# A decoder layer with a mixture of experts: the experts' outputs added into an accumulator in memory instead of stored in two halves

## The chip, the cores and the metric

The kernel runs on one core of a Trainium2 chip. The metric is the device time of one execution in microseconds (us). The core has five engines that run their own instruction streams and wait for each other on semaphores: TensorE (PE: matrix products, with its weight load PEld), VectorE (DVE), ScalarE (ACT), GpSimd (POOL) and SyncE (SP), which here only issues transfers (DMAs). POOL issues DMAs too, above all the indirect ones, whose row addresses come from a tile of indices. SBUF is the on-chip memory with 128 partitions.

## The reference

The input is x, 32 batches of 112 rows of 256 numbers (3584 rows, `NT`), and a context of 32 x 375 rows. A self-attention layer, a cross-attention layer with two subtracted softmaxes, and a mixture of experts follow each other. After each of them its input is added to its output and the sum is normalised to mean 0 and variance 1 per row (`_layernorm`, no weights). Only the last of them matters here:

```
h = normalised rows after cross-attention                      # [3584, 256]
scores = h @ gate_w.T                                          # 8 experts
mult1, mult2, idx = top-2 choice with two weights per row
y[row] = sum over the 2 chosen experts e of  mult_e * (silu(h @ w1[e].T) * (h @ w3[e].T)) @ w2[e].T
out = layernorm(h + y)
```

So each row of the output is a sum of three rows: h and the outputs of two experts.

## The kernel before

The program has four stages, one after another, with a barrier of all engines and a clearing of semaphores between them (`Phase.close`).

`front` computes self-attention, the first normalisation and the projections of the cross-attention, and leaves them in memory.

`cross` goes through the 32 batches. Each batch takes 24 steps (`PARTS`); the order is written out by hand, with tables that say in which step of which batch an engine does a piece. ACT writes the normalised rows h of batch b to `rows[:, b, 0:256]` (line 1005), in step 20 of the loop's batch b + 1, and signals `y_ready`. `rows` is an SBUF tile that lives to the end; beside the 256 numbers of h each row carries its own number (column 256), its first expert and its two weights. POOL scatters every row of a batch twice into the tensor `routed` in memory (line 916), sorted by expert. Rows between the experts' ranges are filled from the tile `pad` (lines 904 to 910), 256 rows by one DMA, nine DMAs in all, which SP issues at the end of the stage (lines 876 and 877); the first eight need a row address that the routing gives last. A padding row carries expert -1, weights 0 and a row number of 7168 or above. SP also feeds the loop: for each batch the two parts of the negated row maxima (`row`, line 858, after ACT's copy in line 978), and the loads of keys and queries (`load`). When c reaches 32, SP loads the first expert's weights into slot 0 of `w` (line 870, 3 MB), to be ready for the next stage.

`experts` works through 35 blocks of 256 sorted rows (two tiles of 128 rows, `BT`). Per block SP loads the rows (line 1403) and the expert's weights (line 1407, 3 MB, into one of two slots, issued once the block before has left that slot). PE turns the rows, multiplies by w1 and w3 in 8 pieces, and by w2 in 8 pieces, each as three half-precision products. DVE works out in `destinations` the share of each row and its destination `dest_i`: row number r for a row whose first choice this expert is, 3584 + r for the second choice, a place behind 7168 for a padding row. ACT scales the result into `y` (line 1465), and POOL scatters it tile by tile to the tensor `y` in memory (line 1427). No two scatters ever write the same row, so nothing orders them. The tile y has two slots, one per block in turn; DVE's `destinations` and ACT's scaling wait for the scatters of the block two before (`y_stored`).

`finish` reads both halves of `y` back, in 4 chunks of 8 batches, with 112 partitions. POOL adds the two halves (line 1628), DVE adds h from `rows` (line 1637) and takes the statistics (lines 1640 and 1644), POOL turns them into a scale and a shift (lines 1618 to 1624, of which 1620 is the power -0.5), ACT applies them (line 1651) and SP stores the chunk (line 1607).

The lines below are those that set the order in the last stage on POOL: the addition of a chunk stands before the statistics of the chunk before.

```
                for c in range(chunks):
                    pool.wait_ge(loaded[c], 32)
                    pool.tensor_tensor(y1[:, c], y1[:, c], y2[:, c], ALU.add).then_inc(half_sum, 1)
                    if c:
                        statistics(c - 1)
                statistics(chunks - 1)
```

## Time and profile before

| what | us |
|---|---|
| median of 3 runs | 1861.12 (1859.83 to 1864.59) |
| the profiled execution, its own time | 1862.62 |
| its span in the trace | 1860.7 |
| stage `finish`, from its first DMA issue to the end | 57.34 |
| PE busy | 1629.8 |
| DVE busy | 1153.1 |
| ACT busy | 915.8 |
| POOL busy | 747.5 |

The first three lines say how long the program takes; the profiled execution is 1.5 us above the median of the timed runs. The busy times are sums over all stages, so they say which engine sets the pace over most of the program (PE), and nothing on a single stage. All times of the trace count from the span's start.

### The profile page before, as it was taken

Reading aid. Unit: us, or ns where it says so; the run is one execution under the profiler, and the core shown is the slowest. Engines: PE = TensorE matmul, PEld = TensorE weight load, DVE = VectorE, ACT = ScalarE, POOL = GpSimd, SP = SyncE. Lnnn points to the kernel's source line nnn. Section 1 sums busy time; section 2 is a strip of 40 time slices with the busy share of each in tenths; the row PEclk is TensorE's granted clock in tenths of the full one; section 3 lists DMA queues with packets and bytes.
Section 4 is the critical chain, followed back from the end, with each engine's and each line's share of the span. In section 5 each row is a group of like instructions: output and inputs, shape, how many; then the busy total and the mean of one; then the engine's idle time right before and its main releaser. Section 6 shows DMA issues by size and latency. Waiting matters only on the chain. (4 is left out here: it accounts for less than half of the span.)

```text
span 1860.7 us, 46590 instructions
## 1 busy us (share of the span) xinstructions
PE 1629.8 (88%) x17724; PEld 1223.2 (66%) x17724; DVE 1153.1 (62%) x2648; ACT 915.8 (49%) x2168; POOL 747.5 (40%) x928
## 2 busy tenths in 40 slices
PE   4899999995999999999999998579999999999950
PEld 2666666663566666666665665368888888888840
DVE  5566666662888887788777888434444444444424
ACT  2344444443466666666666665434444444444423
POOL 6343343322755666765775576301111101111116
PEclk9999999997799999999999999779999999999985
DMA  6666666644444445555554453356555566666637
GB/s 174 186 188 172 177 187 176 181 112 97 136 139 138 131 125 145 145 140 136 147 166 124 132 150 98 127 199 238 224 220 222 223 228 237 238 238 228 220 88 184
DMA packets 204149, 317.11 MB, mean 170 GB/s; under 512 B 60600, under 2 KB 170840, under 8 KB 203928
## 3 DMA queue, kind: packets, MB, share of 16 engines
q1 hardware_dynamic: 188280, 247.16, 44.5%
q0 software_dynamic: 15648, 66.97, 10.2%
q8 instruction: 142, 2.33, 0.5%
q14 instruction: 79, 0.65, 0.1%
HBM read 225.84 MB, written 87.89 MB: 169 GB/s over the span
## 5 line engine op out<-in xcount | busy, mean ns | idle before, releaser
L1165 DVE TENSOR_REDUCE cross_mx<-cross_bank_max 112x2 f32<-112x750 f32 x512 | 460.7, 933 | 119.1 <-PE cross_bank_max L1245 116.4
L996 ACT ACTIVATE cross_probs<-cross_bank_score 125x448 f32<-125x448 f32 x768 | 406.5, 545 | 241.9 <-PE cross_bank_score L1235 238.9
L1556 PE MATMUL experts_bank_h<-experts_x_hi,w 128*128 128x256 f16 x2240 | 373.3, 274 | 1.4 <-DVE experts_x_lo L1477 1.4
L1556 PE MATMUL experts_bank_h<-experts_x_lo,w 128*128 128x256 f16 x1120 | 306.6, 274 | 0.0
L1514 DVE TENSOR_TENSOR experts_hid<-experts_bank_h,experts_gated 128x256 f32<-128x256 f32 x280 | 118.6, 424 | 285.5 <-ACT experts_gated L1453 285.4
L1235 PE MATMUL cross_bank_score<-cqst,ckst 97*125 97x448 f16 x768 | 283.9, 371 | 4.8 <-ACT cross_probs L996 2.4
L1245 PE MATMUL cross_bank_max<-ckst,cqst 96*112 96x375 f16 x1024 | 258.8, 335 | 28.2 <-DVE cross_mx L1165 21.2
L1427 POOL DMA_INDIRECT y<-experts_y,experts_dest_i x70 | 67.2, 960 | 510.1 <-ACT experts_y L1465 499.4
L1556 PEld LDWEIGHTS experts_bank_h<-experts_x_hi,w 128*128 128x128 f16 x2240 | 220.0, 98 | 27.7 <-DVE experts_x_lo L1477 1.8
L1261 PE MATMUL cross_bank_out<-cross_probs,cross_val 125*32 125x112 f32 x6144 | 202.0, 264 | 0.1
L1453 ACT ACTIVATE experts_gated<-experts_bank_h 128x256 f32<-128x256 f32 x280 | 107.5, 384 | 189.9 <-PE experts_bank_h L1556 185.5
L1245 PEld LDWEIGHTS cross_bank_max<-ckst,cqst 96*112 96x112 f16 x1024 | 129.5, 134 | 89.3 <-DVE cross_mx L1165 36.2
L1568 PE MATMUL experts_bank_y<-w,experts_h_hi 128*128 128x256 f16 x1120 | 185.3, 273 | 0.0
L1261 PEld LDWEIGHTS cross_bank_out<-cross_probs,cross_val 125*32 125x32 f32 x6144 | 140.7, 110 | 60.9 <-issue 44.5
L1568 PE MATMUL experts_bank_y<-w,experts_h_lo 128*128 128x256 f16 x560 | 152.6, 273 | 0.0
L925 POOL TENSOR_SCALAR cross_ew_big<-cross_ew 128x512 f32<-128x512 f32 x96 | 143.8, 1498 | 17.9 <-DMA w_halves<-cross_ew_half 14.1
L1235 PEld LDWEIGHTS cross_bank_score<-cqst,ckst 97*125 97x125 f16 x768 | 104.3, 136 | 63.7 <-ACT cross_probs L996 31.2
L447 ACT ACTIVATE front_probs<-front_bank_score 112x448 f32<-112x448 f32 x128 | 69.0, 539 | 124.1 <-PE front_bank_score L605 124.1
L1483 DVE TENSOR_TENSOR experts_h_lo<-experts_hid,experts_h_hi 128x256 f16<-128x256 f32 x280 | 116.8, 417 | 5.2 <-ACT experts_h_hi L1446 3.5
L1556 PEld LDWEIGHTS experts_bank_h<-experts_x_lo,w 128*128 128x128 f16 x1120 | 110.0, 98 | 13.2
L1568 PEld LDWEIGHTS experts_bank_y<-w,experts_h_hi 128*128 128x128 f16 x1120 | 109.6, 98 | 12.7
L1446 ACT ACTIVATE experts_h_hi<-experts_hid 128x256 f16<-128x256 f32 x280 | 114.5, 409 | 6.4 <-DVE experts_hid L1514 6.3
(216 smaller groups left out, 2746.9 us busy)
## 6 DMA issues: line engine op xcount, KB each, us to landing
w<-w_halves SPq DMA_DIRECT2D x35, 3072.0 KB, 11.7
cross_ew<-in_experts POOLq DMA_DIRECT2D x32, 768.0 KB, 5.5
w_halves<-cross_ew_half POOLq DMA_DIRECT2D x32, 768.0 KB
ckst<-cross_k SPq DMA_DIRECT2D x96, 187.5 KB
cross_v<-front_v SPq DMA_DIRECT2D x24, 531.2 KB
cross_val<-cross_v SPq DMA_DIRECT2D x32, 398.4 KB
front_src<-in_ctx_t SPq DMA_DIRECT2D x24, 500.0 KB, 8.9
experts_rows<-routed SPq DMA_DIRECT2D x35, 260.0 KB, 6.3
```

The source lines that it names most:

```text
L925: pool.tensor_scalar(ew_big[:, cols], ew[:, cols], WSCALE, None, ALU.mult).then_inc(ew_big_ready, 1)
L996: nc.scalar.activation(probs[:, e % PROBS], bank_score[e % 2][0:SC, 0:4 * T], ACT.Exp, scale=CROSS_SCALE).then_inc(probs_ready, 1)
L1165: nc.vector.tensor_reduce(mx[:, b % nb, 2 * n:2 * n + 2], bank_max[n % 2][0:T, :, 0:S], AX.X, ALU.max).then_inc(max_read, 1)
L1235: nc.tensor.matmul(bank_score[e % 2][0:SC, 0:pair_w], kst[:, p, g, k * SC:(k + 1) * SC], qst[:, p, g, :], start=True, stop=True).then_inc( ...
L1245: last = nc.tensor.matmul(bank_max[n % 2][0:T, i, 0:S], qst[0:STACK, p, u // 4, (u % 4) * T:(u % 4 + 1) * T], kst[0:STACK, p, u // 4, :], ...
L1261: last = nc.tensor.matmul(bank_out[32 * i:32 * i + 32, at * T:(at + 1) * T], val[:, p, col:col + 32], probs[:, e % PROBS, i * T:(i + 1) * ...
L1446: nc.scalar.activation(h_hi[:, p, f], hid[:, f % 2], ACT.Copy).then_inc(h_hi_ready, 1)
L1453: nc.scalar.activation(gated[:, f % 2], bank_h[f % 4][:, 0:BLOCK], ACT.Silu, scale=1.0 / WSCALE).then_inc(gated_ready, 1)
L1483: nc.vector.tensor_tensor(h_lo[:, p, f], hid[:, f % 2], h_hi[:, p, f], ALU.subtract).then_inc(h_ready, 1)
L1514: nc.vector.tensor_tensor(hid[:, f % 2], bank_h[f % 4][:, BLOCK:2 * BLOCK], gated[:, f % 2], ALU.mult).then_inc(hid_ready, 1)
L1556: last = nc.tensor.matmul(bank_h[f % 4][:, mat * BLOCK:(mat + 1) * BLOCK], w13(p, wh, mat, k, f), xt[:, p, k], start=n == 0, stop=n == len ...
L1568: last = nc.tensor.matmul(bank_y[i][:, 0:D], ht[:, p, f, i * 128:(i + 1) * 128], w2(p, wh, f), start=f == 0 and n == 0, stop=end)
```

## The change

The tensor `y` with its two halves is gone. In its place stands `acc`, with one row for each of the 3584 rows and 256 rows for padding. The stage `cross` stores the normalised rows of each batch in `acc` (a new DMA on SP per batch, behind a wait for `y_ready`), and zeroes the padding rows of `acc` with one more DMA from a wider `pad`. The expert scatters carry `compute_op=ALU.add`, so that each DMA adds its rows to what stands in `acc`. Since the two experts of a row would otherwise collide, POOL waits before each scatter until the one before has landed. `finish` reads one operand, and takes the rows as 128 partitions of 28 neighbouring rows each, 7 to a chunk.

```
 cross, block.sync
                     if on(c + 1):
                         row(c + 1, 0)
+                    if on(c - 1):
+                        b = c - 1
+                        wait(sp, y_ready, b + 1)
+                        sp.dma_start(acc[bass.ts(b, T), :], rows[:, b, 0:D]).then_inc(x_stored, 16)
                     if c == B:
                         wait(sp, ew_stored, 16 * CUTS)
                         sp.dma_start(w[:, 0].rearrange("p q h n -> p q (h n)"),
...
-                    sp.dma_start(routed[bass.ds(at, BLOCK), :].rearrange("(p j) n -> p j n", j=BT), pad[:]).then_inc(padded, 16)
+                    sp.dma_start(routed[bass.ds(at, BLOCK), :].rearrange("(p j) n -> p j n", j=BT), pad[:, :, 0:ROW]).then_inc(padded, 16)
...
+                sp.dma_start(acc[NT:NT + BLOCK, :].rearrange("(p j) n -> p j n", j=BT), pad[:, :, D + 4:ROW + D]).then_inc(padded, 16)
                 sp.wait_ge(w_first, 16)
-                sp.wait_ge(padded, 16 * (EXP + 1))
+                sp.wait_ge(x_stored, 16 * B)
+                sp.wait_ge(padded, 16 * (EXP + 2))
 experts, block.gpsimd
                         wait(pool, y_ready, s.count(BT, 0, i + 1))
-                        pool.indirect_dma_start(y_out[:, :], bass.IndirectOffsetOnAxis(ap=dest_i[:, p, i:i + 1], axis=0),
-                                                y[:, p, i], None).then_inc(y_stored[p], 16)
+                        if i:
+                            wait(pool, y_stored[p], (s.uses() - 1) * (16 * BT) + 16 * i)
+                        else:
+                            wait(pool, y_stored[1 - p], ((s.item() + 1) // 2) * (16 * BT))
+                        pool.indirect_dma_start(acc[:, :], bass.IndirectOffsetOnAxis(ap=dest_i[:, p, i:i + 1], axis=0),
+                                                y[:, p, i], None, compute_op=ALU.add).then_inc(y_stored[p], 16)
 experts, destinations
-                    nc.vector.scalar_tensor_tensor(out=token[:, p], in0=other[:, p], scalar=float(NT), in1=col(0),
-                                                   op0=ALU.mult, op1=ALU.add).then_inc(meta, 1)
...
-                    nc.vector.tensor_tensor(dest_i[:, p], token[:, p], spare[:, p], ALU.add)
+                    nc.vector.tensor_copy(dest_i[:, p], col(0)).then_inc(meta2, 1)
 finish, block.sync
-                    sp.dma_start(y1[:, c], batches(y_in[0:NT, :])[c]).then_inc(loaded[c], 16)
-                    sp.dma_start(y2[:, c], batches(y_in[NT:2 * NT, :])[c]).then_inc(loaded[c], 16)
+                    sp.dma_start(r[:, c], chunk(acc[0:NT, :])[c]).then_inc(loaded[c], 16)
 finish, block.gpsimd (the four small operations stay)
-                    pool.wait_ge(loaded[c], 32)
-                    pool.tensor_tensor(y1[:, c], y1[:, c], y2[:, c], ALU.add).then_inc(half_sum, 1)
 finish, block.vector
-                    dve.wait_ge(half_sum, c + 1)
-                    nc.vector.tensor_tensor(y1[:, c], x[:, c], y1[:, c], ALU.add).then_inc(sum_ready, 1)
-                    dve.wait_ge(sum_ready, c + 1)
+                    dve.wait_ge(loaded[c], 16)
```

On SP the end of `cross` is the first place. `cqst<-cross_neg_mx` is the DMA of the negated maxima, `ckst` and `cqst<-cross_q` the loads of keys and queries, `w<-w_halves` the load of the first expert's weights. Before:

```order
L850 DMA cross_val<-cross_v 125x3x272
L853 DMA cross_x_in<-x1 112x256
L858 DMA cqst<-cross_neg_mx 1x16x112 x4
L870 DMA w<-w_halves 128x4x3072
L875 TENSOR_LOAD cross_pad_row
L875 ISA x2
L876 ISA
L876 DMA routed<-cross_pad 128x520
```

With the change:

```order
L854 DMA cross_x_in<-x1 112x256
L859 DMA cqst<-cross_neg_mx 1x16x112
L872 DMA acc<-rows 112x256
L859 DMA cqst<-cross_neg_mx 1x16x112 x2
L872 DMA acc<-rows 112x256
L859 DMA cqst<-cross_neg_mx 1x16x112
L872 DMA acc<-rows 112x256 x2
L875 DMA w<-w_halves 128x4x3072
L880 TENSOR_LOAD cross_pad_row
L880 ISA x2
L881 ISA
L881 DMA routed<-cross_pad 256x1x260
```

A store of a batch's rows now stands between the two halves of the maxima's DMAs of each batch, and the last two of them, with their waits for ACT, stand ahead of the weight load. The padding DMAs are cut into 256 pieces of 260 numbers instead of 128 pieces of 520.

On POOL the second place is the last stage. Before, its middle reads:

```order
L1628 TENSOR_TENSOR finish_y1<-finish_y1,finish_y2 112x2048 x2
L1618 TENSOR_TENSOR finish_var<-finish_mv,finish_consts 112x8
L1620 TENSOR_TENSOR finish_rstd<-finish_var,finish_consts 112x8
L1622 TENSOR_TENSOR finish_var<-finish_mv,finish_rstd 112x8
L1624 TENSOR_TENSOR finish_shift<-finish_var,finish_consts 112x8
L1628 TENSOR_TENSOR finish_y1<-finish_y1,finish_y2 112x2048
```

With the change:

```order
L1613 MEMSET finish_consts 128x7 x3
L1617 TENSOR_TENSOR finish_var<-finish_mv,finish_consts 128x7
L1619 TENSOR_TENSOR finish_rstd<-finish_var,finish_consts 128x7
L1621 TENSOR_TENSOR finish_var<-finish_mv,finish_rstd 128x7
L1623 TENSOR_TENSOR finish_shift<-finish_var,finish_consts 128x7
```

The four large additions are gone from between the groups of small operations.

## Rows read from the trace of the kernel before

**Rows 1.** windows: stretch, its length, busy time of each engine, clock, DMA share

```profile
1200.00:1800.00 600.00, 569.49 (x5184) 510.28 (x5184) 275.65 (x947) 244.87 (x666) 71.44 (x76) 0.97 0.58 216
1803.36:1860.70 57.34, 0.00 (x0) 0.00 (x0) 22.58 (x68) 16.05 (x32) 32.85 (x23) 0.50 0.75 192
```

**Rows 2.** chain of waits in the last stage: start, us, what

```profile
1804.94 15.14 DMA finish_y<-y
...
1820.15 4.50 POOL finish_y L1628
```

**Rows 3.** timeline, last stage: start, us, engine, line, operation

```profile
1842.43 2.29 DVE L1637 TENSOR_TENSOR finish_y<-rows,finish_y 112x2048 f32<-112x2048 f32 x1 [3.14 <-POOL finish_y L1628]
1842.64 3.59 POOL L1620 TENSOR_TENSOR finish_rstd<-finish_var,finish_consts 112x8 f32<-112x8 f32 x1
1844.76 2.71 DVE L1640 BATCH_NORM_STATS2 finish_stats<-finish_y 112x6 f32<-112x256 f32 x8
...
1846.83 7.96 ACT L1651 ACTIVATE finish_y<-finish_y,finish_shift,finish_rstd 112x256 f32<-112x256 f32 x16 [4.81 <-POOL finish_shift L1624]
1847.50 0.64 DVE L1644 BATCH_NORM_AGGREGATE finish_mv<-finish_stats 112x2 f32<-112x6 f32 x8
...
1848.51 1.64 POOL L1620 TENSOR_TENSOR finish_rstd<-finish_var,finish_consts 112x8 f32<-112x8 f32 x1
...
1850.50 0.20 POOL L1624 TENSOR_TENSOR finish_shift<-finish_var,finish_consts 112x8 f32<-112x8 f32 x1
```

**Rows 4.** DMA issues: count, KB each, median us to landing

```profile
w<-w_halves SPq DMA_DIRECT2D x35, 3072.0 KB, 11.7
...
finish_y<-y SPq DMA_DIRECT2D x8, 896.0 KB, 14.8
...
out<-finish_y SPq DMA_DIRECT2D x4, 896.0 KB, 5.0
routed<-cross_pad SPq DMA_DIRECT2D x9, 260.0 KB, 3.0
...
y<-experts_y,experts_dest_i POOLq DMA_INDIRECT x70, 6.7
```

**Rows 5.** landing times of line 1603 alone

```profile
DMA to landing us min/median/max: 6.1/13.6/15.2
```

**Rows 6.** windows in the middle of transfers

```profile
1504.00:1509.00 5.00, 5.00 (x48) 4.54 (x46) 3.53 (x17) 2.70 (x9) 0.43 (x1) 1.00 1.00 391
1813.00:1820.00 7.00, 0.00 (x0) 0.00 (x0) 2.29 (x1) 0.00 (x0) 4.49 (x1) 0.50 1.12 257
```

**Rows 7.** the expert scatters in the whole trace

```profile
L1427 POOL DMA_INDIRECT y<-experts_y,experts_dest_i x70: 954/959/997, 1243.7 to 1793.9; - x70
```

**Rows 8.** the last two scatters and their landing

```profile
1792.59 0.96 POOL L1427 DMA_INDIRECT y<-experts_y,experts_dest_i  x1 [13.50 <-ACT experts_y L1465]
1793.85 0.96 POOL L1427 DMA_INDIRECT y<-experts_y,experts_dest_i  x1 [0.30 <-issue]
...
DMA to landing us min/median/max: 2.4/2.4/2.4
```

**Rows 9.** timeline of ACT in one batch of the cross stage

```profile
893.22 0.59 ACT L1005 ACTIVATE rows<-cross_r,cross_small 112x256 f32<-112x256 f32 x1
...
899.55 0.24 ACT L978 ACTIVATE cross_neg_mx<-cross_bank_step 16x112 f16<-16x112 f32 x1
```

**Rows 10.** timeline at the end of the cross stage, SP and ACT

```profile
1170.34 0.59 SPq L870 DMA_DIRECT2D w<-w_halves  x1
1204.17 8.42 SPq L876 DMA_DIRECT2D routed<-cross_pad  x8
1212.63 0.44 SPq L877 DMA_DIRECT2D routed<-cross_pad  x1
...
1194.96 0.60 ACT L1005 ACTIVATE rows<-cross_r,cross_small 112x256 f32<-112x256 f32 x1 [4.79 <-POOL cross_small L952]
```

**Rows 11.** the fill of pad

```profile
459.00 0.52 POOL L904 MEMSET cross_pad<- 128x520 f32 x1
```

More of the change, by code:

```diff
@@ L1342, in _, with experts @@
                             rank(n)
-def experts(nc, routed, weights, w, table_i, table_f, y_out):
+def experts(nc, routed, weights, w, table_i, table_f, acc):
     with ExitStack() as ctx:
@@ L1675, in decoder @@
         w = ctx.enter_context(nc.sbuf_tensor("w", [128, 2, CUTS, 2, CUT], F16))
[L1676 to L1678 removed]
+        cross(nc, a, cross_k, cross_q, cross_v, x1, w_halves, routed, acc, rows, table_i, table_f, w, ckst, cqst)
+        experts(nc, routed, w_halves, w, table_i, table_f, acc)
+        finish(nc, acc, a["out"])
 def kernel(x, ctx_1024, L0_attn_Wq, L0_attn_bq, L0_attn_Wk, L0_attn_bk, L0_attn_Wv, L0_attn_bv, L0_attn_Wo, L0_attn_bo,
```

80 lines of the change are left out of this document (33 added, 47 removed).

## Prediction

> **What bounds the kernel now.** I read the windows first, because the change touches three stages with different limits. In the experts' stage PE is busy for 569.49 of 600 us [rows 1]: there nothing but PE counts, as long as the weights, the rows and the free slots of y come in time. In the last stage PE does nothing, DVE is busy for 22.58 us, POOL for 32.85 us and ACT for 16.05 us of 57.34 [rows 1], so no engine fills it; its length is that of a chain. The chain of waits shows which: first 15.14 us for the first two pairs of loads, then POOL's large addition of 4.50 us [rows 2], and from there POOL without a pause. The timeline gives one round: the addition (4.50), then the four small operations, whose power takes 3.59 us while DVE adds h (2.29 us), and 1.64 us in the last chunk, where DVE has nothing left [rows 3]. With the three other small operations of 0.20 us and the gaps a round is about 8.9 us, and three follow each other; ACT and the last store end the stage. ACT does 16 activations in 7.96 us, the last ending at 1846.83 + 7.96 = 1854.79; a store of a chunk lands 5.0 us after its issue [rows 4], at 1859.8, and the stage ends at 1860.7, which is 0.9 us later.
>
> **What the change removes: the last stage worked out anew.** Count from the first DMA issue.
>
> *Load.* A chunk is again 896 KB. The first load of the old stage landed after 6.1 us [rows 5], a store of the same size after 5.0 us [rows 4]. The pieces are now 7 KB instead of 1 KB. Large pieces moved at 391 GB/s inside a weight load (6 KB pieces), the old loads at 257 GB/s [rows 6]. I take 5.5 us for the first chunk, with 5.0 and 6.1 as bounds; the next ones follow every 2.35 to 3.57 us (917,504 bytes by either rate).
>
> *DVE.* Eight statistics take 2.71 us and eight aggregations 0.64 us [rows 3]: 0.34 and 0.08 us each, so 7 and 7 take 2.95 us. DVE's addition (2.29 us, four times) is gone.
>
> *POOL.* The power starts at 1848.51, 0.37 us after DVE's last aggregation ended (1847.50 + 0.64), and the last small operation ends at 1850.70 [rows 3]: 2.56 us from DVE's end to POOL's end. Whether the power stays at 1.64 us beside DVE's statistics is to be asked. In the row of 3.59 us it started at 1842.64; DVE's addition ended at 1844.72 and the statistics ran from 1844.76 on. What is left behind the addition's end is 1.51 us, about the undisturbed time. So the addition stops POOL and the statistics don't. If they did, the power would take 1.64 + 2.4 us, POOL 5.0 us per chunk, and the stage would be longer by 3 x (5.0 - 3.5) + 2.4 = 6.9 us. The Trainium skill ("SBUF — State Buffer", Who interferes with whom) says the same of the two kinds: a VectorE instruction with two SBUF inputs holds off a GpSimd instruction that reads SBUF, one with a single input doesn't; by that rule the 6.9 us stay out.
>
> *ACT.* 7.96 / 16 = 0.50 us each, 3.5 us per chunk, 14.0 us for four. That is longer than DVE's 2.95 and POOL's 2.5 per chunk and not shorter than a load even at the old rate (3.57, against 3.5), so ACT sets the pace from the first chunk on.
>
> Sum: 5.5 + 2.95 + 2.56 + 0.15 (an allowance for two hand-overs) + 14.0 + 5.0 (last store) + 0.9 = 31.1 us instead of 57.34. **Saved: 26.2 us**; with the bounds of the load and of the rates, 25 to 27.
>
> The Trainium skill ("DMA: Bandwidth & Descriptors", Anatomy of one DMA — SWDGE (gpsimd) path) gives a DMA as 2.0 us plus its bytes at 436 GB/s, that is an estimate of 4.1 us for a chunk. By it the stage would save another 1.4 + 0.9 = 2.3 us. The rows show 5.0 and 6.1 for this size in this kernel, and I go by them.
>
> **What it adds, first: the scatters one at a time.** The 70 scatters run from 1243.7 to 1793.9 [rows 7]; less 1.26 us for the second of a pair [rows 8], 34 periods take 548.9 us, so a block is 16.14 us. A scatter lands after 6.7 us in the median [rows 4], because both of a block are issued together with the next weight load, which is in flight for 11.7 us [rows 4]; the last pair, with no load beside it, landed after 2.4 us [rows 8]. Now the second waits for the first. In a block 6.7 + some 4 us is well under 16.14. Behind POOL's waiting scatter only the next scatters are queued; DVE's `destinations` and ACT's scaling wait for scatters of two blocks back. So in the middle of the stage this costs nothing; PE covers it. If that cover is gone, each us by which a pair exceeds the period costs 34 us.
>
> At the end nothing covers it. The last pair started at 1792.59 and 1793.85 and was in memory at 1796.25 [rows 8]. One after the other they need 2 x 2.4 + 0.1 from 1792.59, to 1797.5: 1.2 us more. What an adding scatter costs no row shows. From below it is a plain one, factor k = 1. From above, one that reads the old rows first and then writes is two plain ones, k = 2. I take 1.3, nearer to the plain one, because the bytes (128 KB) are a small part of the 2.4 us and the reads need not wait for each other. The end then moves to 1792.59 + 6.3 = 1798.9: **2.7 us later**, between 1.2 and 6.1.
>
> The weights need a look as well: a load is issued when the block before ends and is needed one block later, 16.14 us, and takes 11.7. The adding scatters read another 256 KB per block, 0.7 us at 391 GB/s. Slack 4.4 us, cost 0. DVE has two operations fewer in a block; DVE is not the bound there, gain 0.
>
> **Second: the stage before.** In a batch SP now waits for y_ready, which comes at 893.81, and issues one DMA; what stands behind it on SP is the next part of the maxima, which ACT gives only at 899.79 [rows 9]. 5.5 us are left, so the 32 stores cost nothing while that holds; their price without cover would be their issue, 32 x 0.44 us as in the ninth padding DMA [rows 10], 14 us. Their 3.7 MB are spread over the stage's 32 batches.
>
> The end of the stage is different. The first weight load was issued at 1170.34; it now stands behind the wait for the last batch's rows, which ACT ends at 1195.56 [rows 10]. Started at about 1196.1 and with its 11.7 us it lands near 1208. The padding DMAs start at 1204.17 and the ninth is issued at 1212.63 [rows 10]; it lands after 3.0 us [rows 4], at about 1215.6. So the weights are still in time, but three padding DMAs now queue behind the load. The tenth DMA costs at least its issue, 0.44 us as the ninth. If the DMA engines are the limit there, it costs its 266 KB at 257 GB/s, 1.0 us, and the three queued ones (0.8 MB) up to 2.5 us more. **I take +1.5 us**, between 0.4 and 3.5.
>
> The fill of pad (0.52 us [rows 11]) doubles. It stands ahead of nothing but POOL's wait for constants, and costs nothing.
>
> **Sum.** -26.2 + 2.7 + 1.5 = -22.0 us. The profiled execution took 1862.62 us, so this one would take 1840.6; it lies 1.5 us above the median. Against the median: 1861.12 - 22.0 = **1839.1 us**.
>
> **Rivals.**
>
> 1. *The serial chain of scatters fills the block, and the kernel gets slower.* The chain runs 11.7 us of a period under the weight load, at 6.7 k us per scatter, and 4.44 us without, at 2.4 k. It completes (11.7 / 6.7 + 4.44 / 2.4) / k = 3.6 / k scatters per period, and needs two. Up to k = 1.8 that costs nothing. Beyond, a period grows by x = (2 k - 3.6) x 2.4 us, which adds up as waits of ACT and DVE, and so of PE, or as scatters left over at the end. It eats the 22 us at x = 0.65, k = 1.93. At k = 2 it is 34 x 0.96 = 33 us, and with 6.1 at the end the time is 1861 - 26 + 1.5 + 33 + 6 = 1875 us. If the rows of one scatter went one after another, each with a round trip of its own (8 rows on each of 16 engines, 2.4 us each, 19 us), it would be far over 2000. For it: the chain is new, and its price is in no row. Against it: the bytes are few. The Trainium skill ("DMA: Bandwidth & Descriptors", Two DMAs through the same engine are not ordered) tells of a second adding packet that read old data when it followed the first at once, so the engine overlaps them; no run here shows that yet. Chance 0.09 slower than 0.3%, and 0.04 for a k so near 1.9 that nothing is left to measure.
> 2. *The last stage gains less.* POOL is held off by the statistics after all, or the loads compete with the stores: +4 to +9 us, 1843 to 1848. The remainder of 1.51 us speaks against it. Chance 0.10.
> 3. *PE loses time in the experts' stage or in the cross stage through more DMA traffic.* A weight load that lands 4.4 us later would be needed. With 0.1 us per block, 3 us; 1842. Chance 0.07, inside the range.
>
> **How the numbers follow.** The forecast has 0.70, with its own range 1834 to 1844 (bounds: -27 + 1.2 + 0.4 and -25 + 6.1 + 3.5, the latter two rarely together). Rivals 2 and 3 carry the range to 1848; the rest of rival 1 leaves 0.13 outside. Range 1833 to 1849. 0.3% is 5.6 us, about what the three runs' spread lets one tell from no change. Faster: 0.70 + 0.10 + 0.07 = 0.87. Same 0.04, slower 0.09.
>
> **What the next profile would show.** The last stage at about 31 us, POOL's power at 1.6 us in all chunks, ACT without a pause between the chunks; the second scatter of a block waiting on its first, the last pair some 3 us apart, and a block still 16.14 us. The cross stage ends 1 to 2 us later, with the weight load issued near 1196. The prediction is wrong if the period of the scatters is above 16.2 us, if PE waits for the weights or for ACT at a block's start, or if ACT waits between chunks of the last stage.

## The result and the profile after

| | before | changed |
|---|---|---|
| median, us (4 runs each) | 1862.42 (1859.83 to 1864.59) | 1835.58 (1832.80 to 1838.25) |
| repeat (9 and 5 runs) | 1859.56 (1856.66 to 1866.20) | 1838.02 (1832.89 to 1840.60) |
| span of the profiled execution | 1860.7 | 1835.8 |

The ratio is 0.9856, with a 95% interval of 0.9833 to 0.9879; in the repeat it is 0.9885 (0.9866 to 0.9904). By the medians the change makes the kernel faster by 26.8 us, and by 21.5 us in the repeat.

To see where the time went I cut both traces at the same events: the first DMA of `cross`, the first padding DMA, the first load of `experts_rows`, the start of ACT's last scaling into y, and the first load of the last stage. The columns are the stretches between these events: "loop" is the work on the batches in `cross`, "pads" runs from the first padding DMA to the first load of the experts' rows, "experts" from there to ACT's last scaling, "tail" from ACT's last scaling to the first load of the last stage, and "finish" is the last stage.

```
run              front    loop  pads  experts   tail  finish    span
before           455.4   748.8  14.0    573.5   11.7   57.34  1860.7
changed          457.1   745.8  17.7    573.2   13.4   28.61  1835.8
difference        +1.7    -3.0  +3.6     -0.3   +1.7   -28.7   -24.9
```

The stages that the change touches give -28.7 + 3.6 + 1.7 - 0.3 = -23.7 us. The rest, +1.7 - 3.0, comes back below the table of the experiments.

**The last stage.** These are the windows of the experts' stage and of the last stage (columns as in [rows 1]):

```profile
1200.00:1800.00 600.00, 568.82 (x5180) 509.48 (x5180) 269.53 (x870) 244.87 (x666) 113.44 (x76) 0.97 0.66 219
1807.19:1835.80 28.61, 0.00 (x0) 0.00 (x0) 11.50 (x56) 13.86 (x28) 8.58 (x19) 0.50 0.64 257
```

PE is as busy in the experts' stage as before (568.8 against 569.5 us). The last stage is half as long, and POOL works 8.58 us in it instead of 32.85. This is the chain that ended last, in that stage:

```profile
1807.19 4.75 DMA finish_r<-acc
...
1811.96 2.40 DVE finish_stats L1630 x7
...
1817.52 8.95 ACT finish_y L1639 x18
```

One load of 4.75 us stands where 15.14 us of loads stood [rows 2], and POOL's addition is gone. The timeline of the same place, to be read beside [rows 3]:

```profile
1814.87 2.35 DVE L1630 BATCH_NORM_STATS2 finish_stats<-finish_r 128x6 f32<-128x256 f32 x7
...
1815.39 1.53 POOL L1619 TENSOR_TENSOR finish_rstd<-finish_var,finish_consts 128x7 f32<-128x7 f32 x1
...
1817.52 13.86 ACT L1639 ACTIVATE finish_y<-finish_r,finish_shift,finish_rstd 128x256 f32<-128x256 f32 x28 [23.28 <-POOL finish_shift L1623]
1817.75 2.35 DVE L1630 BATCH_NORM_STATS2 finish_stats<-finish_r 128x6 f32<-128x256 f32 x7
...
1818.19 1.49 POOL L1619 TENSOR_TENSOR finish_rstd<-finish_var,finish_consts 128x7 f32<-128x7 f32 x1
```

POOL's power takes 1.53 and 1.49 us, although DVE's statistics overlap it in both cases (1814.87 to 1817.22, 1817.75 to 1820.10). ACT runs for 13.86 us without a pause, and every chunk's shift is ready before ACT comes to it: ACT sets the pace.

**The scatters.** The DMA issues of the changed kernel (columns as in [rows 4]):

```profile
w<-w_halves SPq DMA_DIRECT2D x35, 3072.0 KB, 11.6
...
acc<-rows SPq DMA_DIRECT2D x32, 112.0 KB, 2.0
finish_r<-acc SPq DMA_DIRECT2D x4, 896.0 KB, 7.4
out<-finish_y SPq DMA_DIRECT2D x4, 896.0 KB, 3.5
routed<-cross_pad SPq DMA_DIRECT2D x9, 260.0 KB, 4.1
...
acc<-experts_y,experts_dest_i POOLq DMA_INDIRECT x70, 3.9
...
acc<-cross_pad SPq DMA_DIRECT2D x1, 256.0 KB, 3.3
```

The weight load lands as soon as before (11.6 against 11.7 us). The median of 3.9 us for the scatters mixes two kinds: in the middle of the stage the first of a pair, issued beside a weight load, lands after about 8.5 us, the second after 3.8 us. The view of line 1436 alone, the adding scatter, gives its count and duration in ns, then the wait of POOL for a landing, then the landing times:

```profile
L1436 POOL DMA_INDIRECT acc<-experts_y,experts_dest_i x70: 1551/1551/1791, 1245.8 to 1799.0; - x70
...
  DMA acc<-experts_y,experts_dest_i: 269.5, 35
...
DMA to landing us min/median/max: 3.6/3.9/9.6
```

The instruction takes 1.55 us where the plain one took 0.96 [rows 7]. POOL waits 269.5 us in 35 times for the first of a pair, 7.7 us each, and only POOL itself waits for these landings. In the middle of the stage a pair reads as follows; the bracket is POOL's idle time before the instruction and what ended it:

```profile
1504.22 1.55 POOL L1436 DMA_INDIRECT acc<-experts_y,experts_dest_i  x1 [4.88 <-ACT experts_y L1474]
1513.42 1.55 POOL L1436 DMA_INDIRECT acc<-experts_y,experts_dest_i  x1 [7.65 <-DMA acc<-experts_y,experts_dest_i]
```

It is 9.2 us from the first to the second. The whole row of 70 scatters takes 553.2 us (1245.8 to 1799.0) and, less 4.42 us for the last pair's own distance, 34 periods of 16.14 us, as before. At the end of the stage:

```profile
1794.61 1.55 POOL L1436 DMA_INDIRECT acc<-experts_y,experts_dest_i  x1 [9.62 <-ACT experts_y L1474]
1799.03 1.55 POOL L1436 DMA_INDIRECT acc<-experts_y,experts_dest_i  x1 [2.88 <-DMA acc<-experts_y,experts_dest_i]
1807.20 0.18 POOL L1613 MEMSET finish_consts<- 128x7 f32 x3 [6.61 <-POOLq L55]
```

**The end of `cross`.** SP's timeline, to be read beside [rows 10]:

```profile
1194.36 0.31 SPq L872 DMA_DIRECT2D acc<-rows  x1
1194.72 0.43 SPq L875 DMA_DIRECT2D w<-w_halves  x1
1202.92 11.02 SPq L881 DMA_DIRECT2D routed<-cross_pad  x8
1213.98 0.62 SPq L882 DMA_DIRECT2D routed<-cross_pad  x1
1214.64 0.63 SPq L883 DMA_DIRECT2D acc<-cross_pad  x1
```

The weight load went out at 1194.72, 8.2 us ahead of the first padding DMA, where I had expected 8.1 us (1196.1 and 1204.17). The eight padding DMAs took 11.02 us to issue instead of 8.42, the ninth 0.62 instead of 0.44, and the tenth 0.63. In the middle of the loop the new store and the next maxima, beside ACT's rows in [rows 9]:

```profile
893.96 0.32 SPq L872 DMA_DIRECT2D acc<-rows  x1
899.95 0.51 SPq L859 DMA_DIRECT2D cqst<-cross_neg_mx  x1
```

The store's issue is over at 894.28, and SP then issues nothing until ACT has given the next maxima, at 899.93.

### The profile page after: what moved, and what is told of

Same layout as the page of the kernel before. It is cut to its first block and busy times, and to the rows that moved or that the text cites. A ratio compares the mean times of both kernels' runs of the same rounds, so it can differ in the third digit from the quotient of the medians.

```text
span 1835.8 us, 46564 instructions
## 1 busy us (share of the span) xinstructions
PE 1628.7 (89%) x17724; PEld 1223.3 (67%) x17724; DVE 1135.1 (62%) x2566; ACT 913.5 (50%) x2164; POOL 766.3 (42%) x924
## 5 line engine op out<-in xcount | busy, mean ns | idle before, releaser
L1436 POOL DMA_INDIRECT acc<-experts_y,experts_dest_i x70 | 109.7, 1568 | 470.9 <-DMA acc<-experts_y,experts_dest_i 269.5
L1559 PEld LDWEIGHTS experts_bank_h<-experts_x_lo,w 128*128 128x128 f16 x1120 | 109.9, 98 | 13.2
## 6 DMA issues: line engine op xcount, KB each, us to landing
w<-w_halves SPq DMA_DIRECT2D x35, 3072.0 KB, 11.6
```

The source lines that it names most:

```text
L1436: pool.indirect_dma_start(acc[:, :], bass.IndirectOffsetOnAxis(ap=dest_i[:, p, i:i + 1], axis=0), y[:, p, i], None, compute_op=ALU.add).th ...
L1559: last = nc.tensor.matmul(bank_h[f % 4][:, mat * BLOCK:(mat + 1) * BLOCK], w13(p, wh, mat, k, f), xt[:, p, k], start=n == 0, stop=n == len ...
```

## The experiments

Times of stages are from the profiled executions, cut as above:

```
run               front    loop  pads  experts   tail  finish    span
e1_wait_only      459.8   745.0  14.1    572.7   13.2   56.72  1861.5
e2_plain          457.9   745.8  17.4    573.1   13.2   28.71  1836.1
e3_w_early        457.1   752.2  17.0    573.6   13.6   28.64  1842.1
e7_stores_only    455.2   743.9  15.3    572.7   11.6   57.98  1856.7
e4_pad_whole      454.2   744.6  15.2    572.5   13.4   28.49  1828.4
e5_rows_1k        457.6   743.4  17.4    572.8   13.6   34.33  1839.1
e6_three_adds     458.3   745.4  17.4    665.8   20.9   29.07  1936.9
e10_dve_helps     455.1   747.4  14.8    572.8   13.4   25.29  1828.8
e11_plain_71      454.9   748.7  13.7    573.2   11.7   56.81  1859.0
e12_add_71        456.0   742.5  17.8    573.0   13.5   28.62  1831.4
e13_after_again   454.0   744.9  17.3    573.1   13.3   28.48  1831.1
e14_helps_again   456.7   753.4  14.7    572.9   13.4   25.31  1836.4
```

This table answers the open rest above. The code of front is the same in all fourteen kernels, and still front takes 454.0 to 459.8 us, so its +1.7 us is the scatter of single executions. The loop takes 745.0 to 748.8 us in the three kernels without the stores of h, 742.5 to 745.8 in the eight with them, and 747.4 to 753.4 in the three that also load the weights early (e3, e10, e14). That could look like an effect of the code, but the granted clock of TensorE goes with it. In the loop the clock stands at the lower of its two levels, 1.2 GHz, for 59.3 us before and 52.9 us in the changed kernel, 47.1 us in e5 (743.4 us), and 66.2 and 67.3 us in e3 and e14, the two longest loops. A straight line through all fourteen profiles, an estimate, gives 0.50 us of loop for each us at the lower level. By it the kernels before and changed should differ by 3.2 us, and they differ by 3.0. Single loops lie up to 2.0 us off the line, but none of the three groups is more than 0.3 us off on average. And e1, whose loop is that of the kernel before, takes 745.0 us, with 52.1 us at the lower level. So no effect of the code on the loop is shown. Why the clock is low for longer in one execution than in another, or whether something else lengthens the loop and lowers the clock together, stays open.

### Only the wait between the scatters

The kernel before, with POOL's two waits of the change and its plain scatters:

```diff
 experts, block.gpsimd
                         wait(pool, y_ready, s.count(BT, 0, i + 1))
+                        if i:
+                            wait(pool, y_stored[p], (s.uses() - 1) * (16 * BT) + 16 * i)
+                        else:
+                            wait(pool, y_stored[1 - p], ((s.item() + 1) // 2) * (16 * BT))
                         pool.indirect_dma_start(y_out[:, :], ...
```

> The kernel before, with one thing of the change: POOL waits before each scatter until the one before has landed. The scatters are plain, to separate rows. In the middle of the experts' stage I expect nothing: a block stays at 16.1 us, with the second scatter some 6.8 us behind the first. The stage's end is what the run is for. In the kernel before, POOL's drain (the instruction with which it ends its part of a stage) took 5.77 us, in the changed kernel 3.40 us. Theory A, that the drain is long because two scatters were issued close together: it falls to about 3.4 us here; the last scatter lands 1.2 us later, the drain is 2.4 us shorter, so the last stage starts 1.2 us EARLIER against ACT's last y than before (10.8 us behind its start instead of 12.0). Theory B, that the drain ends a fixed 8 us behind the last scatter's issue: the last stage starts about 1.2 us later (13.2 us). The total: no change beyond 2 us by either.

Measured: 1863.78 us (1857.89 to 1867.56, 10 runs), ratio to before 1.0019 (1.0003 to 1.0035), that is 0.6 to 6.5 us more. The experts' stage is as long as before; the tail grew by 1.5 us, to 13.2 us. That is the number of theory B, and theory A (10.8 us) is out: the drain took 5.77 us here too. Here is POOL's timeline at the end of the stage. The last row is its first instruction of the next stage, with its idle time in brackets:

```profile
1792.48 0.96 POOL L1431 DMA_INDIRECT y<-experts_y,experts_dest_i  x1 [11.62 <-ACT experts_y L1469]
1795.64 0.96 POOL L1431 DMA_INDIRECT y<-experts_y,experts_dest_i  x1 [2.20 <-DMA y<-experts_y,experts_dest_i]
1804.79 0.18 POOL L1617 MEMSET finish_consts<- 112x8 f32 x3 [8.19 <-POOLq L55]
```

In the kernel before that last row reads:

```profile
1803.37 0.18 POOL L1613 MEMSET finish_consts<- 112x8 f32 x3 [8.55 <-POOLq L55]
```

The second scatter starts 3.16 us after the first (before 1.26), so the last landing moves by 1.9 us, and POOL's idle time after it is 8.2 instead of 8.6 us. The order alone costs only the tail, as far as these runs can tell.

### The change without the adding

The changed kernel with plain scatters into `acc`. It leaves the sum out: the output's rows then come from the result of one expert only, without h.

```diff
-                                                y[:, p, i], None, compute_op=ALU.add).then_inc(y_stored[p], 16)
+                                                y[:, p, i], None).then_inc(y_stored[p], 16)
```

> The changed kernel with plain scatters (no compute_op=ALU.add), so each row of acc ends up holding only the output of one expert; the waits stay. It prices the adding. The changed kernel's adding scatters show 1.55 us on POOL each and land after 3.7 us alone and 8.6 us beside a weight load; here I expect 0.96 us, 2.4 and 6.7 us as in the kernel before. If my factor k (1.3 assumed) was right in kind, only the end of the experts' stage moves: two scatters at 2.4 instead of 3.8 us land 2.8 us earlier, and by theory A of the drain (its length follows the number of scatters issued close together) the total falls by 2.8 us; by theory B (a fixed 8 us behind the last issue) by 1.4 us. Rival: the adding also loads the DMA engines so that weights or rows come late; then the block's period, 16.14 us, would fall here. I expect it unchanged to 0.02 us.

Measured: 1838.16 us (1836.45 to 1842.47, 4 runs), ratio to before 0.9898 (0.9874 to 0.9923), not told apart from the changed kernel. The period of a block is 16.14 us, as expected. The landing times of its scatters are:

```profile
DMA to landing us min/median/max: 2.4/5.0/7.4
```

The adding ones have 3.6/3.9/9.6 us. Alone at the stage's end it is 2.4 against 3.7 and 3.8 us: adding costs 1.3 us more per scatter, a factor of about 1.55, and 0.6 us of it is POOL's instruction. In the tail the two kernels nevertheless differ by only 0.2 us, where theory A expected 2.8 and theory B 1.4 us, though from the first scatter of the last pair to the last landing it takes 4.42 + 3.80 = 8.2 us with adding and 3.17 + 2.4 = 5.6 without. Something gives that time back; see the drain below.

### The weight load ahead of the last stores

```diff
 cross, block.sync (the changed kernel)
+                    if c == B - 1:
+                        wait(sp, ew_stored, 16 * CUTS)
+                        sp.dma_start(w[:, 0]...)            # as below, moved here
                     if on(c - 1):
                         ...
-                    if c == B:
-                        wait(sp, ew_stored, 16 * CUTS)
-                        sp.dma_start(w[:, 0]...)
```

> The changed kernel with the load of the first expert's weights issued one batch earlier, ahead of the last two stores of rows, as in the kernel before. In the changed kernel it was issued at 1194.7 and was in flight when the padding DMAs began; from the first padding DMA to the next stage's first load it took 17.7 us instead of 14.1. If the queue behind the weight load is the cause, this falls by 2 to 2.6 us, to 15.1 to 15.7 us (the tenth DMA and the smaller pieces stay). If the smaller pieces of the padding DMAs are the cause (260 numbers instead of 520), it stays above 17 us. Total: 2.3 us faster than the changed kernel, or the same.

Measured: 1836.97 us (1832.76 to 1843.87, 4 runs), ratio to before 0.9879 (0.9855 to 0.9903). The stretch from the first padding DMA to the experts' rows went from 17.7 to 17.0 us only; in the other kernels with the same code there it takes 17.3 to 17.8 us. So the queueing of the padding behind the weight load, which I had taken for most of the cost, is the small part of it.

### Only the stores of h

The kernel before, with a DMA per batch into an otherwise unused tensor `acc`, in the place where the change has it:

```diff
 cross, block.sync
+                    if on(c - 1):
+                        b = c - 1
+                        wait(sp, y_ready, b + 1)
+                        sp.dma_start(acc[bass.ts(b, T), :], rows[:, b, 0:D]).then_inc(x_stored, 16)
                     if c == B:
```

> The kernel before, with the 32 stores of the normalised rows to a tensor that nobody reads added in the cross stage, with their waits on SP, and nothing else. The weight load of the first expert stands behind the last store, as in the changed kernel. My reading: the stores are covered, the loop of the cross stage (from its first DMA to the first padding DMA, 748.8 us before, 745.8 us in the changed kernel) stays within 746 to 750 us, and the 3.0 us by which the changed kernel was shorter there are scatter between executions. Rival: the stores really make the loop faster by holding SP's other DMAs back; then 746 us or less shows here as well. The end of the stage, first padding DMA to the next stage's first load, grows from 14.1 us to 15 to 16 us by the weight load alone. Total: 0 to +2 us.

Measured: 1858.71 us (1853.89 to 1863.07, 10 runs), ratio 0.9996 (0.9978 to 1.0014). The stores cost nothing that can be measured, with an interval of -4.1 to +2.6 us. The profiled loop takes 743.9 us, which is what the rival named (746 us or less). But the total doesn't show the stores making the kernel faster, and the lower clock lasts 51.0 us in this loop and 59.3 us in the one before, which makes 4 us at the 0.50 us estimated above. No gain by the stores is shown. The stretch of the padding takes 15.3 us, 1.3 us more than before: that is what the later weight load costs there without the small pieces. Single kernels with the code of before have 13.7 to 14.1 us.

### Padding from whole pieces

The changed kernel, with `pad` at its old width and a tile of zeros of its own for `acc`:

```diff
-        pad = ph.sb("pad", [128, BT, ROW + D], F32)
+        pad = ph.sb("pad", [128, BT, ROW], F32)
+        zero = ph.sb("zero", [128, BT, D], F32)
...
-                    sp.dma_start(routed[...], pad[:, :, 0:ROW]).then_inc(padded, 16)
+                    sp.dma_start(routed[...], pad[:]).then_inc(padded, 16)
```

> The changed kernel with the padding rows in a tile of their own again, so that each padding DMA moves 128 pieces of 520 numbers instead of 256 of 260; the zeros for acc stand in a second tile. From the first padding DMA to the next stage's first load it took 14.1 us before, 17.7 us in the changed kernel and 17.0 us with the weight load issued early, so the queue behind the weight load is worth 0.7 us at most. If the small pieces are the cause, it falls to 14.9 to 15.7 us here (the tenth DMA stays). If it is the tenth DMA and the weight load together, it stays above 17. A look at one profile; the total tells nothing at this size.

Measured: 1830.15 us (one run). SP's timeline at the place of the changed kernel's rows above:

```profile
1198.82 9.42 SPq L882 DMA_DIRECT2D routed<-cross_pad  x8
1208.28 0.43 SPq L883 DMA_DIRECT2D routed<-cross_pad  x1
1208.75 0.45 SPq L884 DMA_DIRECT2D acc<-cross_zero  x1
```

Eight DMAs take 9.42 us to issue instead of 11.02, and the ninth 0.43 instead of 0.62. The stretch is 15.2 us: 2.5 of the 3.6 us were the pieces (2.1 to 2.6 by the scatter of this stretch). The wide `pad` makes two pieces of 1040 B out of each of 2080 B.

### The last stage with one operand, in the old layout

The changed kernel; `finish` takes the chunks as before, 112 partitions with 8 rows of 1 KB each.

```diff
-    n = NT // 128 // chunks
+    n = B // chunks
...
-        chunk = lambda a: a.rearrange("(p c i) n -> c p i n", c=chunks, i=n)
+        chunk = lambda a: a.rearrange("(c i t) n -> c t i n", c=chunks, i=n)
```

> The changed kernel with the last stage's rows laid out as before: 112 partitions, 4 chunks of 8 rows, pieces of 1 KB in the loads and the stores; still one operand. It splits the gain of the last stage (57.3 to 28.6 us) into operand and layout. By the terms of my prediction: 6.1 (first load) + 3.35 (DVE) + 2.56 (POOL) + 0.15 + 16.0 (ACT, 32 rows) + 5.0 (last store) + 0.9 = 34.1 us. So the operand is worth 23.2 us of 28.7 and the layout 5.5 us. Rival: with 1 KB pieces the loads of the later chunks come so late that ACT waits for them; then 36 us or more, and the stage would be bound by DMA.

Measured: 1840.88 us (one run), last stage 34.33 us, where 34.1 was expected. Its chain begins with

```profile
1804.77 6.52 DMA finish_r<-acc
```

and ACT works in it for

```profile
1817.41 15.83 ACT L1639 ACTIVATE finish_y<-finish_r,finish_shift,finish_rstd 112x256 f32<-112x256 f32 x32 [25.75 <-POOL finish_shift L1623]
```

that is 32 activations instead of 28. So of the 28.7 us that the last stage lost, 23.0 belong to the operand and to the additions of POOL and DVE (57.34 - 34.33), and 5.7 to the layout: 1.8 on the first load, 2.0 on ACT, 0.4 on DVE's first chunk, and 1.4 on the last store (4.9 us there against 3.5).

### Three adding scatters in a block

The changed kernel, where each block's first tile is scattered twice, each scatter waiting for the one before; the outputs of those rows count twice.

```diff
+                        for q in range(2 - i):
+                            if i or q:
+                                wait(pool, y_stored[p], (s.uses() - 1) * 48 + 16 * (i + i + q))
+                            else:
+                                wait(pool, y_stored[1 - p], ((s.item() + 1) // 2) * 48)
-                        pool.indirect_dma_start(acc[:, :], ...
+                            pool.indirect_dma_start(acc[:, :], ...
```

> The changed kernel with the first tile's scatter of each block issued twice, one after the other (the expert outputs of that tile are counted twice), so three serial adding scatters per block instead of two. It tests the sentence that the chain of scatters costs nothing until it fills a block, with the formula of rival 1. Measured in the changed kernel: 8.6 us per scatter beside a weight load (11.6 us of a period), about 3.9 us without one, with the hand-over. Three per period need 11.6 / 8.6 + (T - 11.6) / 3.9 = 3, T = 18.0 us instead of 16.14. The experts' stage grows by 33 x 1.9 = 60 us (50 to 70), seen as waits of DVE or ACT for the scatters. Rival: the scatters of a block overlap the weight load less than the formula has it, because PE's wait delays the next weight load too, and the chain just fits: then under 10 us. The drain of POOL at the stage's end: with plain scatters it took 5.77 us in all four kernels, with adding ones 3.40 us in both, whatever stood between the scatters. If it goes by the kind of scatter, 3.40 us again; if by their number (70 so far), something else.

Measured: 1935.28 us (1929.04 to 1942.22, 4 runs), ratio to before 1.0393 (1.0346 to 1.0441). The sign and the mechanism are those of rival 1, the size is not: the experts' stage grew by 92.6 us over the changed kernel, where about 60 were expected, and the tail by 7.5 us, because POOL's scatters run further behind ACT and POOL's drain (below) is 2.9 us longer. POOL's timeline in the middle:

```profile
1517.22 1.55 POOL L1437 DMA_INDIRECT acc<-experts_y,experts_dest_i  x1 [8.05 <-DMA acc<-experts_y,experts_dest_i]
1521.94 1.69 POOL L1437 DMA_INDIRECT acc<-experts_y,experts_dest_i  x1 [3.17 <-DMA acc<-experts_y,experts_dest_i]
1526.73 1.55 POOL L1437 DMA_INDIRECT acc<-experts_y,experts_dest_i  x1 [3.10 <-DMA acc<-experts_y,experts_dest_i]
1536.43 1.55 POOL L1437 DMA_INDIRECT acc<-experts_y,experts_dest_i  x1 [8.15 <-DMA acc<-experts_y,experts_dest_i]
```

A block now takes 19.21 us, in three steps of 4.72, 4.79 and 9.70. My formula had 3.9 us for a scatter without a weight load and 8.6 us beside one, hand-over included. But the hand-over (landing, semaphore, POOL's next issue) adds about 0.9 us to the landing of 3.8. The waits say who pays (us in total, number of waits, the longest):

```profile
POOL acc L1437 <- DMA acc<-experts_y,experts_dest_i: 461.3, 98, 9.3
...
DVE experts_first L1501 <- DMA acc<-experts_y,experts_dest_i: 147.2, 29, 7.1
...
PE experts_bank_h L1560 <- DVE experts_hid L1518: 63.3, 28, 4.2
```

DVE waits for the scatters of two blocks back, as the prediction said of rival 1, and PE waits for DVE. So the cover is real and it has an end: two serial adding scatters fit into 16.14 us (9.2 us, and about 4.4 for a step without a weight load, as in the last pair: 13.6 us), a third doesn't.

### What POOL does at the end of the experts' stage

The trace also holds an instruction that the views don't count as busy: POOL's DRAIN, with which it ends its part of a stage, ahead of the barrier. This table is read from the trace's records, with its start counted from the start of the last scatter:

```
run              scatters   starts after, us   takes, us
before           70 plain         2.58           5.772
e7_stores_only   70 plain         2.58           5.772
e1_wait_only     70 plain         2.60           5.772
e2_plain         70 plain         2.59           5.772
changed          70 adding        3.98           3.403
e13_after_again  70 adding        3.93           3.403
e6_three_adds   105 adding        4.01           6.302
e11_plain_71     71 plain         2.57           5.853
e12_add_71       71 adding        3.95           3.444
```

It starts just after the last scatter has landed (2.42 us after its start before, 3.80 in the changed kernel), and its length doesn't depend on how far apart the last scatters stood (1.26 us before, 3.16 in e1). Two kernels were made to tell whether the number of scatters counts, or only their kind. Each issues block 0's first tile once more and waits for it:

```diff
                         wait(pool, y_ready, s.count(BT, 0, i + 1))
+                        if s.item() == 0 and i == 0:
+                            pool.indirect_dma_start(y_out[:, :], ..., y[:, p, i], None).then_inc(extra, 16)
+                            pool.wait_ge(extra, 16)
```

> The kernel before with one plain scatter more, at the very start of the experts' stage: the first tile of block 0 is scattered twice (the second one writes the same rows with the same values). The end of the stage is untouched. POOL's drain there took 5.77 us in all kernels with 70 plain scatters, however close the last ones stood. Theory N: the drain's length depends on how many DMAs POOL has issued in the program; then it changes here, though nothing near it did. Theory K: it depends on the kind of scatter and on what stands last; then it is 5.77 us again.

Measured: 1860.76 us (one run), drain 5.853, 0.081 us longer; 5.772 / 70 is 0.082. In the second kernel the rows of that tile count twice:

> The changed kernel with one adding scatter more at the start of the experts' stage (the first tile of block 0 is counted twice). The drain took 3.40 us with 70 adding scatters and 6.30 us with 105. Theory N (number of DMAs issued): it differs from 3.40 us, and the way from the last scatter's landing to the last stage moves with it. Theory K (kind, and what stands last): 3.40 us.

Measured: 1833.09 us (one run), drain 3.444, 0.041 us longer. One plain scatter adds 0.08 us, one adding scatter 0.04, so the number counts, and the kind sets the price of each. The 105 adding ones are longer than that price gives (3.403 + 35 x 0.041 = 4.8, measured 6.3), so it isn't proportional throughout. Nor is the price the same for all that POOL issues: at the end of `cross`, where it has issued 64 scatters and 64 plain DMAs, its drain takes 1.86 us in all fourteen kernels. Whether the scatters of the stage count or those of the whole program these runs can't tell, since both rose together. What POOL does in the drain stays open.

### Whole pieces, early weights, seven chunks, and DVE helping ACT

The sum of what the runs pointed to: e3 and e4 together, 7 chunks of 4 rows (in each of the 128 partitions) in the last stage, and one row of four scaled by DVE, which has idle time there.

```diff
 finish
-    chunks = 4
+    chunks = 7
 block.vector, behind the statistics of chunk c, for chunk d = c - 1
+                        dve.wait_ge(shift_ready, d + 1)
+                        for i in range(n - on_dve, n):
+                            nc.vector.tensor_scalar(y[:, d, i], r[:, d, i], rstd[:, d, i:i + 1],
+                                                    shift[:, d, i:i + 1], ALU.mult, ALU.add).then_inc(dve_ready, 1)
 block.scalar
-                    for i in range(n):
+                    for i in range(n - on_dve):
```

> A version to beat both: the changed kernel with the whole padding tile and the early weight load, and the last stage in 7 chunks of 4 rows, of which ACT scales 3 and DVE 1. In the changed kernel ACT is the last stage's pace (13.9 us for 28 rows). Here ACT has 21 rows, 10.4 us, and DVE 28 x 0.42 (statistics) + 7 x 0.3 = 13.9 us, so DVE sets the pace. First load of 512 KB 4.2, DVE 13.9 less what it does behind the last chunk, POOL 2.5, last rows 1.5, last store (512 KB) 2.8, end 0.9: 25 us instead of 28.6. Padding: 15 instead of 17.7 us. Sum: 5.5 to 6.5 us faster than the changed kernel, 1829.5 us. Rival: POOL's four small operations, now seven times 2.5 us = 17.5 us, become the pace of the last stage; then 4.2 + 1.7 + 17.5 + 1.5 + 2.8 + 0.9 = 28.6 us, and nothing is gained there.

Measured: 1831.10 us (1828.11 to 1837.27, 6 runs), ratio to before 0.9841 (0.9809 to 0.9873). The last stage takes 25.3 us. One round of its timeline:

```profile
1815.63 1.39 DVE L1635 BATCH_NORM_STATS2 finish_stats<-finish_r 128x6 f32<-128x256 f32 x4
1815.64 1.01 POOL L1624 TENSOR_TENSOR finish_rstd<-finish_var,finish_consts 128x4 f32<-128x4 f32 x1
...
1817.06 0.38 DVE L1638 BATCH_NORM_AGGREGATE finish_mv<-finish_stats 128x2 f32<-128x6 f32 x4
1817.24 1.58 ACT L1650 ACTIVATE finish_y<-finish_r,finish_shift,finish_rstd 128x256 f32<-128x256 f32 x3 [0.37 <-POOL finish_shift L1628]
1817.35 0.38 DVE L1642 TENSOR_SCALAR finish_y<-finish_r,finish_rstd,finish_shift 128x256 f32<-128x256 f32 x1
...
1817.65 1.40 DVE L1635 BATCH_NORM_STATS2 finish_stats<-finish_r 128x6 f32<-128x256 f32 x4
```

ACT's three rows take 1.58 us of a round of some 2.1, so ACT no longer sets the pace: DVE does, which works without a pause, with 1.40 + 0.38 + 0.38 us. It and the changed kernel had so far run on different occasions, so both ran once more side by side.

> The changed kernel once more, on the same chip as the next one, so that the two are compared side by side. 1835.6 us, within 3 us; the stages as in its first profile except the cross stage's loop, which moved between 743 and 752 us from execution to execution in all kernels.

> The version with the whole padding tile, the early weight load and the last stage in 7 chunks with DVE's help, once more beside the changed kernel. Its stages gave 25.3 us for the last stage (28.6 in the changed kernel) and 14.8 us for the padding (17.7). Together 6.2 us. So 6 us faster than the changed kernel, 3 to 8 by the scatter of the runs. Rival: what was gained in the cross stage's end is lost in its loop, since the early weight load shares the DMA engines with the loads of the last batches: then 3 us.

Measured: the changed kernel 1838.02 us (1832.89 to 1840.60, 5 runs), ratio 0.9885 (0.9866 to 0.9904); this one 1831.77 us (1826.74 to 1838.15, 5 runs), ratio 0.9843 (0.9826 to 0.9860). It is 6.2 us faster, as the stages say: 25.3 for 28.5 and 14.7 for 17.3 are 5.8. Its profiled loop (753.4 us) is the longest of all, and e3 (752.2), with the same early weight load, is next, which could have been a cost of that load, as the rival had it. But the load is issued 33.8 us before the first padding DMA, and from ACT's write of the rows of batch 29, still earlier, to that DMA it takes 41.0 to 41.4 us in all fourteen kernels. The loops differ before that point. Besides, the profiled execution of this kernel was the slowest of its five (1838.15 us), and that of the changed kernel the fastest of its five (1832.89 us). No cost of the early load is shown, and the total came 6.2 us faster, not 3.

## Why the prediction was right, and which terms were off

The prediction had 1839.1 us and a sum of -22.0; measured are -26.8 and in the repeat -21.5 us by the medians, and -23.7 in the stages that the change touches. The sum came so close partly by luck: the last stage saved 2.5 us more than said, and the end of `cross` cost 2.1 us more. The lower end of the forecast's own range, 1834 us, does not follow from the bounds given with it, -27 + 1.2 + 0.4, which make 1835.7 us. Term by term:

- **Last stage**: -28.7 instead of -26.2 us. The chain was the one described (load, DVE, POOL, ACT without a pause, store), and ACT's 13.86 us stood at 14.0. Off were both transfers: the load took 4.75 us for 5.5 and the last store 3.5 for 5.0. DVE's first chunk took 2.96 us, as said. I had taken the old store's 5.0 us over unchanged while I counted the larger pieces for the load. The Trainium skill ("DMA: Bandwidth & Descriptors", Anatomy of one DMA — SWDGE (gpsimd) path) fits a DMA as 2.0 us plus its bytes at 436 GB/s, an estimate of 4.1 us for either. Its fit is for DMAs issued from GpSimd, and SP issues these. The runs show 4.75 us in and 3.5 out with 7 KB pieces, and 6.5 in and 4.9 out (e5) with 1 KB pieces: the estimate lies between the first two and below the other two.
- **POOL beside the statistics** (rival 2): 1.48 to 1.53 us in all chunks, the last included, where no statistics run beside it. It isn't held off, and the rival is out.
- **The experts' stage in the middle**: nothing, as said; the period is 16.14 us. e6 shows where the cover ends, and rival 1's mechanism with it. Rival 1's formula left out the hand-over of 0.7 to 0.9 us per scatter, which would have moved its point of decision, not its verdict here.
- **End of the experts' stage**: +1.7 instead of +2.7 us, and this by two errors that nearly cancel. From the first scatter of the last pair to the last landing it takes 4.42 + 3.80 = 8.2 us instead of 3.7 [rows 8], 4.5 us more, because adding costs a factor of 1.55, not 1.3, and the hand-over takes 0.7 us, not 0.1; so the last pair stands 4.4 us apart and not some 3. And POOL's drain, which the prediction didn't know of, became 2.4 us shorter. The last 0.4 us lie between the drain's end and the first load, 1.15 us before and 0.77 in the changed kernel. The range of 1.2 to 6.1 held it.
- **End of `cross`**: +3.6 instead of +1.5 us, just above its bound of 3.5. The step that failed is "three padding DMAs now queue behind the load", taken as the main cost: the later load costs 0.7 us by e3 and 1.3 us by e7, and 0.4 to 0.5 us by e4 (15.2) against e10 and e14 (14.8 and 14.7). The larger part, 2.5 us (e4), is the cutting of the padding into pieces of 1040 B, which stood in the order's rows and which I priced at nothing.
- **The stores of h**: nothing beyond the noise, alone in e7.
- **PE slowed by more traffic** (rival 3): PE 568.8 us busy of 600, weight loads at 11.6 us; out.

## What to carry to other kernels

A sum of partial results can be left to an adding scatter if something else covers the time of the serial chain: count landing plus hand-over, not landing alone, against the period, and price the last link of the chain at the stage's end apart, because nothing covers it there. When a tile is widened to serve two DMAs, look at what becomes of the pieces of the first; here that cost about 2.5 us, and a separate tile gave it back. Once a stage's large operations are gone, see which engine now sets its pace and give part of its work to an idle one.

## What the runs showed of the hardware that I had not expected

- An adding scatter of 128 rows of 1 KB: 1.55 us of POOL, 3.7 to 3.8 us to landing alone, and about 8.5 us beside a 3 MB load. The plain one, in the same order (e2): 0.96 us, 2.4 us, and up to 7.4 us.
- POOL's drain at the end of the experts' stage grows with the scatters that it has issued: 5.77 us for 70 plain ones, 5.85 for 71; 3.40 for 70 adding ones, 3.44 for 71, 6.30 for 105. Whether they count by stage or by program is open.
- The same 896 KB: 4.75 us in and 3.5 us out with 7 KB pieces, 6.5 us in and 4.9 us out with 1 KB pieces (e5). The same 260 KB cut into 256 pieces instead of 128 cost 0.2 us more per DMA in the issue.
- In the loop of `cross` the fourteen profiles have TensorE's clock at its lower level, 1.2 GHz, for 47.1 to 67.3 us, and loops of 742.5 to 753.4 us. The loop is longer by about 0.50 us for each us at that level (an estimate from these fourteen). So a difference of a few us between two single profiles there says nothing on the code before their clocks are compared.
